# Audio tower kernel: values weighed in 12 double sessions a body, a ring of four probability groups, another order of the single bank's fills

## The reference

```python
def _tdnn_forward(x, W, b, gamma, beta):          # 16 x 746 x 128
    y = relu(einsum('blf,of->blo', patches(x, 5), W) + b)
    return (y - mean(y)) * rsqrt(var(y) + BN_EPS) * gamma + beta
...
scores = jnp.einsum('bhqd,bhkd->bhqk', qp, kp) * scale       # 8 heads of 16
probs = jax.nn.softmax(scores, axis=-1)
attn = jnp.einsum('bhqk,bhkd->bhqd', probs, vp)
...
h = _L0_tok_ref(x, ...)
h = h + _L0_attn_ref(_layernorm(h), ...)                     # 746 x 746 per head
h = h + _L0_ffn_ref(_layernorm(h), ...)                      # top-1 of 8 experts
```

## Time and profile before

| what | value |
|---|---|
| median of 3 runs | 1467.63 us (1467.03 to 1468.56) |
| the profiled execution's own time | 1461.96 us |
| its span, first to last instruction | 1460.1 us |
| PE busy | 1339.3 us, 92% |
| DVE busy | 1083.7 us, 74% |
| ACT busy | 978.0 us, 67% |
| one full body (bodies 1 to 13) | 67.17 us |

### The profile page before, as it was taken

The page is one execution under the profiler, slowest core; times in us unless marked ns, Lnnn a source line. Parts: engine busy times, 40 slices in busy tenths (PEclk is TensorE's granted clock), DMA queues, the critical chain, the costliest instruction groups (busy, mean ns, idle before and its releaser), DMA issues.

```text
span 1460.1 us, 31108 instructions
## 1 busy us (share of the span) xinstructions
PE 1339.3 (92%) x9928; PEld 757.9 (52%) x9928; DVE 1083.7 (74%) x3005; ACT 978.0 (67%) x2735; POOL 589.2 (40%) x538
## 2 busy tenths in 40 slices
PE   6738899999999999999999999999999985799996
PEld 3423344454545454454545454544444432799996
DVE  4329878788887888888888878888888613477775
ACT  1321487777878787878777787878776782477774
POOL 0004223353535343444435363434442122456665
PEclk9999799999999999999999999999999996799998
DMA  3041522415040514223150505142232041333331
GB/s 52 1 87 28 76 65 33 91 28 111 23 102 31 88 50 68 68 51 82 37 110 8 117 17 101 45 74 65 54 79 40 16 138 39 104 105 105 105 105 53
DMA packets 70139, 96.78 MB, mean 66 GB/s; under 512 B 14637, under 2 KB 60029, under 8 KB 70016
## 3 DMA queue, kind: packets, MB, share of 16 engines
q1 hardware_dynamic: 61232, 75.73, 25.0%
q0 software_dynamic: 7872, 18.54, 4.4%
q10 hardware_dynamic: 912, 0.94, 0.3%
HBM read 56.72 MB, written 39.00 MB: 66 GB/s over the span
## 4 chain that ended last, share of the span: by engine, by line
PE 79%; DVE 11%; ACT 3%; DMA 2%; POOL 2%; issue 2%; SPq 1%; POOLq 0%; DVEq 0%; ACTq 0%
PE psum L1076 18%; PE psum L1094 17%; PE psum L1108 14%; DVE half_max L869 7%; PE psum L1140 6%; PE psum L1150 6%; PE psum L983 3%; PE psum L1042 3%; PE psum L1012 3%; PE psum L995 2%; PE psum L1020 2%; PE psum L1036 2%; PE psum L1048 1%; ACT p_ring L635 1%; DVE stats L734 1%
## 5 line engine op out<-in xcount | busy, mean ns | idle before, releaser
L869 DVE TENSOR_REDUCE half_max<-psum 128x1 f32<-128x373 f32 x1536 | 771.3, 537 | 186.5 <-PE psum L1108 184.7
L635 ACT ACTIVATE p_ring<-psum 128x373 f32<-128x373 f32 (+1 forms) x1536 | 688.0, 494 | 273.6 <-PE psum L1094 190.9
L1108 PE MATMUL psum<-k_rows,q_rows 96*128 96x373 bf16 x1536 | 506.0, 332 | 26.5 <-DMA k_rows<-k_parts_dram 20.7
L1094 PE MATMUL psum<-q_rows,k_rows 98*128 98x373 bf16 (+1 forms) x1536 | 496.7, 328 | 3.7 <-ACT p_ring L635 2.9
L1076 PE MATMUL psum<-p_ring,values 128*32 128x373 f32 (+1 forms) x3072 | 321.1, 490 | 2.4 <-ACT o_un L648 2.1
L1094 PEld LDWEIGHTS psum<-q_rows,k_rows 98*128 98x128 bf16 (+1 forms) x1536 | 156.6, 103 | 297.1 <-ACT p_ring L635 192.3
L525 POOL DMA_INDIRECT routed_rows_dram<-rows,pos_i x96 | 96.0, 1000 | 363.8 <-DVE tok_id L863 178.8
L1108 PEld LDWEIGHTS psum<-k_rows,q_rows 96*128 96x128 bf16 x1536 | 154.1, 100 | 115.9 <-DVE half_max L869 44.4
L565 POOL DMA_INDIRECT out_dram<-p_ring,slot_id x102 | 121.1, 1187 | 84.2 <-DVE p_ring L962 67.0
L1076 PEld LDWEIGHTS psum<-p_ring,values 128*32 128x32 f32 (+1 forms) x3072 | 61.1, 108 | 104.9 <-issue 61.8
L549 POOL TENSOR_TENSOR rstd<-var_eps,minus_half 128x6 f32<-128x6 f32 x16 | 21.6, 1347 | 162.5 <-DVE var_eps L746 162.5
(11 more groups left out here) (156 smaller groups left out, 1600.8 us busy)
## 6 DMA issues: line engine op xcount, KB each, us to landing
q_rows<-q_parts_dram SPq DMA_DIRECT2D x192, 93.2 KB, 3.2
k_rows<-k_parts_dram SPq DMA_DIRECT2D x192, 93.2 KB, 4.5
p_ring<-routed_rows_dram SPq DMA_DIRECT2D x102, 130.0 KB
q_parts_dram<-q_part SPq DMA_DIRECT2D x16, 559.5 KB, 3.0
k_parts_dram<-k_part SPq DMA_DIRECT2D x16, 559.5 KB, 3.0
seq<-in_w_dram SPq DMA_DIRECT2D x1, 2048.0 KB, 8.7
seq<-in_w_dram SPq DMA_DIRECT2D x8, 256.0 KB, 6.5
out_dram<-p_ring,slot_id POOLq DMA_INDIRECT x102
```

Of the source, the lines that this page charges most:

```text
L635: last = nc.scalar.activation(probs[0:kn(kt), G % N_P, j, :], st_of(i, s)[0:kn(kt), 0:HALF], ACT.Exp)
L869: nc.vector.tensor_reduce(half_max[:, s:s + 1], mx_bank[s % N_MX][:, 0:HALF], AX.X, ALU.max)\
L1094: last = nc.tensor.matmul(st_of(i, s)[0:kn(kt), 0:HALF], k_rows[par][0:KM, h, D * kt:D * kt + kn(kt)], q_rows[par][0:KM, h, qh * HALF:(qh ...
L1108: nc.tensor.matmul(mx_bank[s % N_MX][:, 0:HALF], q_rows[1 - par][0:KR, h, D * t:D * (t + 1)], k_rows[1 - par][0:KR, h, half * HALF:(half + ...
```

## The change

`WEIGH_AT` pairs the groups: two key tiles are weighed after step 12 of a pass, two after 20, two after 28. A body thus has 12 sessions of eight matmuls (sixteen instructions) in place of 24 of four. They are 8 steps apart: after steps 4, 12, 20, ... 92. `p_ring` holds four groups, since a group now waits longer. V's first fill goes to the head of the list, and everything in the bank is moved by a few steps; the consumers on ACT and DVE move with the fills.

```diff
-    WEIGH_AT = (7, 11, 15, 19, 23, 28)
+    WEIGH_AT = (12, 12, 20, 20, 28, 28)
-    N_ST, N_MX, N_P = 3, 3, 3
+    N_ST, N_MX, N_P = 3, 3, 4
...
-        FILLS = (("OT0", 0, 6), ("OT0", 1, 10), ("OT1", 0, 14), ("OT1", 1, 18), ("V", 0, 22), ("PROJ", 0, 26),
-                 ("PROJ", 1, 30), ("V", 1, 34), ("MAX1", 0, 38), ("Q", 0, 45), ("Q", 1, 49), ("K", 0, 53), ("K", 1, 57),
-                 ("MAX0", 0, 61), ("LOGIT", 0, 65), ("RANK", 0, 77))
-        BESIDES = {"HTOK": (0, 1, 2, 3, 5, 6), "MT": (16, 17, 18, 24, 25, 26), "XNT": (36, 37, 38, 40, 41, 42),
-                   "XN2T": (50, 51, 53, 54, 56, 57)}
+        FILLS = (("V", 0, 6), ("OT0", 0, 10), ("OT0", 1, 14), ("OT1", 0, 18), ("OT1", 1, 22), ("PROJ", 0, 26),
+                 ("V", 1, 30), ("PROJ", 1, 34), ("MAX1", 0, 38), ("Q", 0, 46), ("Q", 1, 50), ("K", 0, 54), ("K", 1, 58),
+                 ("MAX0", 0, 62), ("LOGIT", 0, 66), ("RANK", 0, 78))
+        BESIDES = {"HTOK": (0, 1, 2, 3, 5, 6), "MT": (17, 18, 19, 25, 26, 27), "XNT": (36, 37, 38, 40, 41, 42),
+                   "XN2T": (54, 55, 57, 58, 59, 61)}
...
-                    if s in (7, 8, 11, 12, 15, 16, 19, 20) and live(i, -1):
-                        normalise(i, i - 1, (s - 7) // 8, (s - 7) % 8 // 4, (s - 7) % 4)
+                    if s in (11, 12, 15, 16, 19, 20, 23, 24) and live(i, -1):
+                        normalise(i, i - 1, (s - 11) // 8, (s - 11) % 8 // 4, (s - 11) % 4)
...
```

More of the change, by code:

```diff
@@ L652, in body @@
                         max_out(i, i, 1, "MAX1")
[L653 to L657, removed]
+                    if s in (47, 48, 51, 52) and live(i, 2):
+                        q_or_k(i, "Q", (s - 47) // 4, (s - 47) % 4)
+                    if s in (55, 56, 59, 60) and live(i, 2):
+                        q_or_k(i, "K", (s - 55) // 4, (s - 55) % 4)
+                    if s == 63 and live(i, 1):
                         max_out(i, i + 1, 0, "MAX0")
-                    if s == 75 and live(i, -1):
+                    if s == 76 and live(i, -1):
                         act.wait_ge(s_rt, (i - 1) * 10 + 7)
@@ L879, in body @@
                         layer_stats(i + 2, s - 10, h_cur, stats, mv, var_eps, s_ln)
-                    if s in (23, 35) and live(i, 1):
-                        bias_values(i, par, s // 35)
+                    if s in (7, 31) and live(i, 1):
+                        bias_values(i, par, s // 31)
                     if s == 26 and is_body(i, FIRST_BODY):
@@ L884, in body @@
                         norm_rows(nc.vector, lambda t: xn[:, t, :], lambda t: h_cur[:, t, :], mv, rstd, s_ln_p)
[L885 to L888, removed]
+                    if s in (27, 35) and live(i, -1):
+                        residual(i, i - 1, s // 35)
+                    if 37 <= s < 43 and live(i, -1):
+                        if s == 37:
                             dve.wait_ge(s_free, fill(i, "PROJ", 1))
-                        layer_stats(i - 1, s - 33, rows, stats2, mv2, var_eps2, s_ln2)
+                        layer_stats(i - 1, s - 37, rows, stats2, mv2, var_eps2, s_ln2)
                     if s == 46 and is_body(i, LAST_BODY):
@@ L897, in body @@
                         split(dve, nc.vector, s_apart_v, i, "K")
[L898 to L903, removed]
+                    if 67 <= s < 75 and live(i, -1):
+                        router(i, i - 1, s - 67)
+                    if 78 <= s < 80 and live(i, -1):
+                        router(i, i - 1, s - 70)
+                    if 80 <= s < 86 and live(i, -1):
+                        ranks(i, i - 1, s - 80)
             run_bodies(dve, body)
```

## The result

| | before | after |
|---|---|---|
| median | 1467.33 us (4 runs, 1466.98 to 1468.56) | 1537.03 us (4 runs, 1533.42 to 1537.58) |
| span of the profiled execution | 1460.1 us | 1535.7 us |
| PE busy | 1339.3 us, 92% | 1352.2 us, 88% |
| a full body | 67.17 us | 70.95 us in seven, 72.50 to 72.59 in six |

The ratio is 1.0468, with a 95% interval of 1.045 to 1.0486. The forecast was 1522 us, with a range of 1480 to 1545: 69.7 us came where 54.7 had been forecast.

The account below looks back on a forecast made before the run. The prediction took PE, the tensor engine, as the bound, with waits for DVE and ACT. Four stretches gave +4.1 us a body, thirteen bodies +53, in all +57: forecast 1522 us, own range 1500 to 1545, stated range 1480 to 1545.

Parts of the forecast that it names:

- The price of a session: At each paired session: second key tile costs 0.67 us, each pairing saves 0.19, twelve save 2.3 us a body.
- The rule of the Trainium skill: In sessions: weight loads overlap matmuls only across row groups; as a rival, pairing saves nothing, 1555 us, chance 0.05.
- Runs of eight steps: Steps 69 to 4: PE waits for maxima banks from a run's fifth step; 20.1 us against 18.5, +1.6.
- Steps 5 to 28: V first, OT later: OT wait goes, first and fourth MT pieces wait for products; 19.7 us against 19.03, +0.7.
- The MT wait: First MT piece, waiting for DVE's product of step 16: 9.6 us after score 5, nominally 7.8.
- the OT fills: In the kernel before: PE waits 2.1 us a body here, for ACT's copy of `o_un`, then DVE's products.
- Steps 29 to 44 and 45 to 68: PROJ and statistics waits: 11.2 becomes 12.0 us, +0.8; Q, K and LOGIT waits: 18.43 becomes 19.4, +1.0.
- The Q wait: Second Q fill, steps 45 to 68: waits 0.9 us for ACT to free the bank, without a session between.
- The sum: A full body: 19.7 + 12.0 + 19.4 + 20.1 = 71.2 us against 67.17, +4.1.
- the one on the clock: Rival, through the bodies: more PE waiting lowers the granted clock to 0.94, 4 us more each, 1575 us; chance 0.03.
- The ends: Body 0 +1 (-1 to +2), body 14 +1.3, body 15 +1 (from -2) us.
- the whole end: After the bodies: the experts were said to stay as they were, with no change in time.

Follow-up runs that it names:

- the cut reductions: Both kernels with each DVE maxima reduction cut to 186 of 373 columns: changed kernel 1444.76 us, kernel before 1433.41 us.
- experiment 4: Kernel before with the whole new order of fills, single sessions, and MT pieces moved later: 1460.67 against 1460.97 us, ratio 1.0001.
- experiment 1: Kernel before with only the sessions paired and a ring of four groups, fills as before: 1498.12 us, ratio 1.0259.
- experiment 3: Changed kernel with MT pieces after steps 21, 22, 23, 29, 30, 31 instead of 17, 18, 19, 25, 26, 27: 1505.61 us, ratio 1.0316.
- experiment 2: Changed kernel with single sessions and three groups restored, leaving only the new order of fills: 1475.29 us, ratio 1.0107 to the kernel before.

## Why the prediction was right, and what it missed

- **The price of a session.** I took 0.67 us for the second key tile, from 0.62 to 0.86. It is 0.63 (1.46 less 0.83), so a pairing saves 0.23 and twelve save 2.8 us, not 2.3. The weight loads are hidden under the passes, as the row of loads had said: of the sixteen of the session above, eight start by 720.78 and the last by 721.41, while its matmuls run on to 722.2. The rule of the Trainium skill (TensorE: Matmul & The Clock Gate, The mechanism; the prediction named a neighbouring section), by which they would not be, does not hold for these sessions.
- **Runs of eight steps.** Forecast 20.1 us for steps 69 to 4, measured 19.95; by parts (body 7) 5.10, 4.86, 4.67 and 5.31, where 5.1, 5.0, 4.7 and 5.3 stood. The 0.455 spacing from the fifth step on is in the timeline, and the cut reductions take the loss away: shown.
- **Steps 5 to 28.** Forecast 19.7, measured 19.47 at full clock. The MT wait of 1.8 us is the one foreseen (nominal 7.8, forecast 9.6 us after score 5). That it is nearly all of the order's cost was not foreseen: 1.14 of 1.16 us with single sessions (experiment 4), 0.9 of 1.4 with paired ones (70.95 less 70.03, and less the 69.57 of experiment 1). One reading was loose: by starts the OT fills of the kernel before wait 1.8 us a body, and 2.2 only with V's first.
- **Steps 29 to 44 and 45 to 68.** Forecast 12.0 and 19.4, measured 11.98 and 19.55. The Q wait of 0.9 us is in the timeline. The order by itself also costs 0.5 there with single sessions, and putting Q, K and what follows back one step removes 0.4 of it; with paired sessions it costs nothing (19.56 without it, 19.55 with it).
- **The sum.** 71.2 forecast, 70.95 measured, where the clock held. **The step that failed is the one on the clock**: I gave it 0.03, as something that would lower the clock through all bodies, and argued from body 14 that waits of PE do not trigger it. In fact single waits of 1.8 us were followed by 3.4 us at half clock in six bodies, about 1.6 us each, 9.6 in all. Body 14 could not show this: its longest single wait is 1.4 us.
- **The ends.** Bodies 0, 14 and 15 were put at +3.3 together and came to +9.4: +2.9, +1.6 and +4.9. Body 15 alone holds 10.2 us at half clock. After the last score, routing the last sequence and the experts took 257.7 us against 249.4. Of these 8.3 us some 3.5 lie between the last score and the last sequence's first PROJ fill, where the clock falls to half in both kernels. The rest is in the experts, where PE waited once for 3.5 us for ACT and the clock fell for 3.4 us. In experiments 1 to 3, which have between them every part of the change, the whole end took 248.5 to 249.3 us; why it was longer in the changed kernel stays open; the prediction had put it at nothing.

Thirteen bodies make 58.7 us, bodies 0, 14 and 15 9.4, the end 8.3, less 0.8 before the first body: 75.6, the difference of the two profiled spans. Against the forecast of 57 the thirteen bodies, had the clock held, came 4 us lower (49.1 against 53), and the clock (9.6), the three bodies at the ends (6.1 more than said) and what follows the last score (8.3) together 24 us higher. The mechanism of the body was right; that the total stayed in the range is owed in part to the range's width, since terms of that size had been put at or near nothing.

## What to carry to other kernels

A long uninterrupted stop of one engine has to be covered by the buffers that the others drain meanwhile. Before saving switches by merging stops, multiply the consumers' spacing by the number of buffers: here 3 x 0.455 = 1.4 us stood against a stop of 1.65, and the single session's stop of 1.03 had been below it. This is an estimate from one kernel; no run changed the number of banks. And before saving anything, look at which waits hide behind the stop that goes: the Q and K fills had used the single sessions as their cover (experiment 1). Where a chain goes through two engines, its length from producer to consumer (here 1.2 us and more from matmul to released transpose, an estimate from the earlier trace rows) is the least distance in the order. MT pieces that stood too near their product cost 1.1 us a body here with single sessions, and 2.5 with paired ones where the clock fell with them.

## What the runs showed of the hardware that I had not expected

- The same PE wait of about 1.8 us was followed by 3.4 us at half clock in six full bodies and by none in seven; with that wait gone (experiment 3) no full body had one. Waits of 0.9 us at the same pieces, in all thirteen bodies of experiment 2, had no fall behind them either. At half clock, in body 15, a paired session is shown 2.71 us long instead of 1.46 (PE's timeline of the changed kernel):

```profile
1260.29 2.71 PE L1076 MATMUL psum<-p_ring,values 128*32 128x373 f32 x16
```

- A float32 session of 32-column matmuls on four column groups goes on into a second set of weights without a gap that the trace shows: the four passes start 0.34, 0.31 and 0.31 us apart, the change of weights between the second and the third, and the second key tile costs 0.63 us, two such distances.
